# Moving the second gate product, the output product and the turn of the next input in an attention stage

## What is computed

```python
H, DK, DV, M = (16, 64, 128, 64)
x = layernorm(x)
q, k, v, g = x @ Wq, x @ Wk, x @ Wv, x @ Wg
s = clip(x @ Ws, -32, 32)
z = cumlogsumexp(s, axis=time);  p = exp(s - z)
# slots' keys: hk_t = hk_(t-1) * exp(z_(t-1) - z_t) + k_t p_t ;  ok_t = q_t . hk_t
pv = softmax(ok)
# slots' values: hv_t = hv_(t-1) * exp(z_(t-1) - z_t) + p_t v_t ;  o_t = pv_t . hv_t
o = o * rsqrt(mean(o * o) + EPS) * g_norm_weight * (g * sigmoid(g))
x_out = x_in + o @ Wo
```

## Time and profile before

| what | value |
|---|---|
| runs | 2952.86, 2950.38, 2964.53 us; median 2952.86 |
| the profiled execution's own time | 2954.36 us |
| its span, first to last instruction | 2952.5 us |
| mean granted TensorE clock over the span | 0.926 |
| TensorE matmuls busy | 2514.7 us, 85% |
| VectorE busy | 1756.5 us, 59% |
| GpSimd busy | 1258.2 us, 43% |
| ScalarE busy | 890.2 us, 30% |

### The profile page before, as it was taken

How to read it: one execution, slowest core, us unless ns; L and a number is a source line. 1 busy time by engine, 2 the same in 40 slices (tenths; PEclk the granted TensorE clock), 3 DMA queues, 4 the chain that set the end, 5 groups by cost and what they waited for, 6 DMA issues and landing times. The chain is left out here.

```text
span 2952.5 us, 46247 instructions
## 1 busy us (share of the span) xinstructions
PE 2514.7 (85%) x17244; PEld 2143.4 (73%) x17244; DVE 1756.5 (59%) x3538; ACT 890.2 (30%) x1886; POOL 1258.2 (43%) x1257
## 2 busy tenths in 40 slices
PE   6466499999999999999999999854654899796998
PEld 5444378888888888888888888754443678675777
DVE  5333267778787777777777777643222444464543
ACT  6222133333333333333333333253221222232322
POOL 2277634554444555555444455412883211242000
PEclk9588799999999999999999999855997899897999
DMA  6699600000000000000000000035995111111110
GB/s 219 172 255 236 132 11 19 5 15 19 19 9 15 15 19 19 5 16 19 19 8 15 16 19 12 3 124 144 217 217 110 61 58 35 43 57 44 36 35 30
DMA packets 210065, 186.21 MB, mean 63 GB/s; under 512 B 29280, under 2 KB 202304, under 8 KB 209344
## 3 DMA queue, kind: packets, MB, share of 16 engines
q1 hardware_dynamic: 180624, 133.83, 15.2%
q0 software_dynamic: 24576, 37.77, 6.9%
q10 hardware_dynamic: 4656, 11.80, 1.3%
HBM read 126.26 MB, written 61.52 MB: 64 GB/s over the span
## 5 line engine op out<-in xcount | busy, mean ns | idle before, releaser
L895 POOL TENSOR_TENSOR a_orstd<-a_ms,minus_half 128x8 f32<-128x8 f32 x64 | 106.3, 1661 | 637.4 <-DVE a_ms L1055 637.4
L1028 DVE TENSOR_TENSOR a_at<-a_psB,causal 128x384 f32<-128x384 f32 x512 | 260.6, 551 | 100.2 <-PE a_psB L1200 100.2
L875 POOL TENSOR_SCALAR a_pick<-a_index,lut_row 128x258 f32<-128x258 int32 x240 | 279.5, 1165 | 24.4
L1048 DVE RECIPROCAL a_rz<-a_rz 128x256 f32<-128x256 f32 x128 | 221.6, 1733 | 0.0
L616 PE MATMUL e_psX<-ident,e_xg 128*128 128x128 f32 x256 | 62.9, 333 | 177.5 <-DMA e_xg<-rows,slot_tok 177.4
L709 DVE TENSOR_TENSOR e_hT<-e_psH,e_sil 128x128 f32<-128x128 f32 x128 | 37.3, 292 | 272.6 <-ACT e_sil L677 272.5
L1578 DVE TENSOR_TENSOR f_hs<-f_psU,f_sil 128x512 f32<-128x512 f32 x96 | 66.2, 690 | 219.8 <-PE f_psU L1403 219.8
L616 PEld LDWEIGHTS e_psX<-ident,e_xg 128*128 128x128 f32 x256 | 32.1, 160 | 225.7 <-DMA e_xg<-rows,slot_tok 221.3
L878 POOL TENSOR_TENSOR a_found<-a_found,a_pick 128x258 f32<-128x258 f32 x240 | 177.6, 740 | 20.0
L1261 PE MATMUL a_psD<-a_v,a_at 128*128 128x128 f32 x1536 | 182.0, 275 | 0.0
L1261 PEld LDWEIGHTS a_psD<-a_v,a_at 128*128 128x128 f32 x1536 | 176.9, 192 | 0.1
(11 more groups left out here) (257 smaller groups left out, 7750.2 us busy)
## 6 DMA issues: line engine op xcount, KB each, us to landing
e_wg<-in_L_ffn_w_gate SPq DMA_DIRECT2D x128, 128.0 KB, 3.4
e_wu<-in_L_ffn_w_up SPq DMA_DIRECT2D x128, 128.0 KB, 3.7
e_wd<-in_L_ffn_w_down SPq DMA_DIRECT2D x128, 128.0 KB, 4.3
rows<-r_row SPq DMA_DIRECT2D x32, 320.0 KB, 3.1
stream_b<-r_zeros SPq DMA_DIRECT2D x11, 384.0 KB, 6.7
stream_c<-rows SPq DMA_DIRECT2D x33, 128.0 KB, 3.2
r_xt<-in_L_attn_hidden_states SPq DMA_DIRECT2D x16, 256.0 KB, 3.9
stream_a<-r_xt SPq DMA_DIRECT2D x16, 256.0 KB, 4.5
```

The lines of the kernel that those rows point to most:

```text
L875: nc.gpsimd.tensor_scalar(pick[:, :, :], index[:, :, :], float(c), w["lut"][:, c:c + 1], ALU.is_equal, ALU.mult).then_inc(picked, 1)
L895: nc.gpsimd.tensor_tensor(out=flat(orstd[:, :, :]), in0=ms[:, :], in1=cst["minus_half"][:, 0:TT * HQ], op=ALU.pow).then_inc(orstd_ok, 1)
L1028: nc.vector.tensor_tensor(out=at[:, h, :], in0=psB[h % 2][:, 0:3 * P], in1=cst["causal"][:, :, :].rearrange("p a i -> p (a i)"), op=ALU.mu ...
L1048: nc.vector.reciprocal(rz[:, a, :], rz[:, a, :]).then_inc(rz_ok, 1)
```

## The change

On TensorE, the turn of the next input goes from behind the first causal scores to between the first gate product and the second slot scores. The second gate product goes to behind the second slot scores, before the value sum. The output product goes from there to between the two pairs of causal scores, writes psC[0] in place of a bank of psA, and waits for the low part of lnT, since the turn also writes psC[0]. The slots' read waits for the adding of the output two rounds back. The gate's wait for that adding and the output's wait for the key go.

On VectorE, the moments of the next input are taken in the round of quarter 1 in place of 2, and the normalising in that of quarter 2 goes from behind the second reciprocal to where the moments stood. The subtraction for the low part goes from between the two gates to between the two reciprocals, and the adding of the output goes from there to behind the second gate.

On ScalarE, the copy of the high part goes from between the two gate tanhs to before the squares. On GpSimd, the 1/sqrt for the input goes from behind the look-ups of quarter 2 to directly behind the sum of the input in quarter 1, ahead of that round's look-ups.

```diff
--- before.py
+++ after.py
@@ -886,9 +886,8 @@
                     more = b + 1 < B
                     if q == 1 and more:
                         add_stream(b + 1)
+                        rstd_of_stream(b + 1)
                     look_up(b, range(4 * q, 4 * q + 4))
-                    if q == 2 and more:
-                        rstd_of_stream(b + 1)
                     if q == 0:
                         accumulator(b)
                     pool.wait_ge(ms_ok, n + 1)
@@ -968,6 +967,8 @@
                     if ahead:
                         key(n + 1)
                         turned_exps(n + 1)
+                        if (n + 1) % QPB == QPB - 1 and n + 2 < N:
+                            high_of_stream((n + 1) // QPB + 1)
                     for t in range(TT):
                         if t == 0:
                             act.wait_ge(ov_ps, n + 1)
@@ -976,8 +977,6 @@
                         nc.scalar.activation(sq[:, t * HQ * DV:(t + 1) * HQ * DV], psD[:, t, :], ACT.Square).then_inc(sq_ok, 1)
                     if ahead:
                         gate_tanh(n + 1, 0)
-                        if (n + 1) % QPB == QPB - 1 and n + 2 < N:
-                            high_of_stream((n + 1) // QPB + 1)
                         gate_tanh(n + 1, 1)
                 high_of_output(N - 1)
 
@@ -1009,13 +1008,13 @@
                                                 in1=oT[:, 0, 2 * a:2 * a + 2, :].rearrange("p a t -> p (a t)"),
                                                 op=ALU.subtract).then_inc(otl_ok, 1)
 
-                def add_output(n, bank):
+                def add_output(n):
 
                     dve.wait_ge(out_ps, n + 1)
                     dve.wait_ge(xacc_ok, n // QPB + 1)
                     if n > 0:
                         dve.wait_ge(acc_ok, n)
-                    nc.vector.tensor_tensor(out=xacc[:, :, :].rearrange("p t d -> p (t d)"), in0=psA[bank],
+                    nc.vector.tensor_tensor(out=xacc[:, :, :].rearrange("p t d -> p (t d)"), in0=psC[0],
                                             in1=xacc[:, :, :].rearrange("p t d -> p (t d)"), op=ALU.add).then_inc(acc_ok, 1)
 
                 def clip(m):
@@ -1086,6 +1085,8 @@
                     nc.vector.scalar_tensor_tensor(out=es[:, :], in0=sm[:, :], scalar=4.0 * EPS, in1=sm[:, :],
                                                    op0=ALU.mult, op1=ALU.mult).then_inc(es_ok, 1)
                     if q == 2 and b + 1 < B:
+                        normalise_stream(b + 1)
+                    if q == 1 and b + 1 < B:
                         moments_of_stream(b + 1)
                     dve.wait_ge(ezt_ps, n + 1)
                     nc.vector.tensor_tensor(out=flat(pzT[:, :, :]), in0=psC[0], in1=flat(rz[:, :, :]), op=ALU.mult).then_inc(pzt_ok, 1)
@@ -1099,12 +1100,9 @@
                     if ahead:
                         running_sum(n + 1, 1)
                         invert(n + 1, 0)
-                    if n > 0:
-                        add_output(n - 1, (n + 1) % 2)
-                    if ahead:
+                        if (n + 1) % QPB == QPB - 1 and n + 2 < N:
+                            low_of_stream((n + 1) // QPB + 1)
                         invert(n + 1, 1)
-                    if q == 2 and b + 1 < B:
-                        normalise_stream(b + 1)
                     dve.wait_ge(ov_ps, n + 1)
                     dve.wait_ge(tg_ok, TT * n + TT)
                     gated_output(n, 1)
@@ -1113,13 +1111,14 @@
                     if ahead:
                         masked(n + 1, (0, 1), at_ps, at_ok)
                         gate(n + 1, 0)
-                        if (n + 1) % QPB == QPB - 1 and n + 2 < N:
-                            low_of_stream((n + 1) // QPB + 1)
                         gate(n + 1, 1)
+                    if n > 0:
+                        add_output(n - 1)
+                    if ahead:
                         masked(n + 1, (2, 3), at_ps, at_ok)
                     squares(n)
                 low_of_output(N - 1)
-                add_output(N - 1, (N + 1) % 2)
+                add_output(N - 1)
 
             @block.tensor
             def _(pe):
@@ -1182,8 +1181,6 @@
                         pe.wait_ge(q_ok, m + 1)
                     else:
                         pe.wait_ge(k_ok, m + 1)
-                        if m > 1:
-                            pe.wait_ge(acc_ok, m - 1)
                     project("g", psA[(1 - m % 2) if t == 0 else m % 2], m, t, HQ * DV, g_ps)
 
                 def turn_exps(m):
@@ -1223,8 +1220,8 @@
 
                 def slots_read(n):
 
-                    if n > 0:
-                        pe.wait_ge(pzt_ok, n)
+                    if n > 1:
+                        pe.wait_ge(acc_ok, n - 1)
                     for a in range(NH):
                         pe.wait_ge(at_ok, HQ * n + 2 * a + 2)
                         for i, (t, j) in enumerate(((0, 0), (1, 0), (1, 1))):
@@ -1271,12 +1268,12 @@
                                                          o2[:, t, h * DV:(h + 1) * DV], ident)
                         mm.then_inc(ot_ps, 1)
 
-                def output(n, bank):
+                def output(n):
 
                     pe.wait_ge(otl_ok, NH * n + NH)
                     for t in range(TT):
                         for h in range(HQ):
-                            mm = split_matmul(nc, psA[bank][:, t * D:(t + 1) * D], [oT[:, part, h, t * P:(t + 1) * P] for part in range(2)],
+                            mm = split_matmul(nc, psC[0][:, t * D:(t + 1) * D], [oT[:, part, h, t * P:(t + 1) * P] for part in range(2)],
                                               [w["o"][part][:, n % QPB * HQ + h, :] for part in range(2)], h == 0, h == HQ - 1)
                     mm.then_inc(out_ps, 1)
 
@@ -1312,23 +1309,22 @@
                     scores_b(n, (0, 1))
                     if ahead:
                         gate(n + 1, 0)
-                    scores_b(n, (2, 3))
-                    if n > 0:
-                        if ahead:
-                            pe.wait_ge(k_ok, n + 2)
-                        else:
-                            pe.wait_ge(tg_ok, TT * n + TT)
-                        output(n - 1, (n + 1) % 2)
-                    over_j(n)
-                    if ahead:
-                        scores_a(n + 1, (0, 1))
                         if (n + 1) % QPB == QPB - 1 and n + 2 < N:
                             turn_stream((n + 1) // QPB + 1)
+                    scores_b(n, (2, 3))
+                    if ahead:
                         gate(n + 1, 1)
+                    over_j(n)
+                    if ahead:
+                        scores_a(n + 1, (0, 1))
+                    if n > 0:
+                        pe.wait_ge(lnTl_ok, min((n + 1) // QPB + (2 if (n + 1) % QPB == QPB - 1 else 1), B))
+                        output(n - 1)
+                    if ahead:
                         scores_a(n + 1, (2, 3))
                 turn_output(N - 1)
                 pe.wait_ge(acc_ok, N - 1)
-                output(N - 1, (N + 1) % 2)
+                output(N - 1)
         clear_semaphores(nc, mem)
 
 
```

More of the change, by code:

```diff
@@ L1314, in _ @@
                         gate(n + 1, 0)
+                        if (n + 1) % QPB == QPB - 1 and n + 2 < N:
+                            turn_stream((n + 1) // QPB + 1)
                     scores_b(n, (2, 3))
-                    if n > 0:
-                        if ahead:
-                            pe.wait_ge(k_ok, n + 2)
-                        else:
-                            pe.wait_ge(tg_ok, TT * n + TT)
-                        output(n - 1, (n + 1) % 2)
+                    if ahead:
+                        gate(n + 1, 1)
                     over_j(n)
@@ L1324, in _ @@
                         scores_a(n + 1, (0, 1))
-                        if (n + 1) % QPB == QPB - 1 and n + 2 < N:
-                            turn_stream((n + 1) // QPB + 1)
-                        gate(n + 1, 1)
+                    if n > 0:
+                        pe.wait_ge(lnTl_ok, min((n + 1) // QPB + (2 if (n + 1) % QPB == QPB - 1 else 1), B))
+                        output(n - 1)
+                    if ahead:
                         scores_a(n + 1, (2, 3))
```

## The result

| | before | after |
|---|---|---|
| median | 2956.86 us (17 runs) | 2945.55 us (17 runs) |
| ratio after/before | | 0.9958, 95% interval 0.9947 to 0.997 |
| span of the profiled execution | 2952.5 us | 2943.7 us |
| mean granted TensorE clock over the span | 0.926 | 0.938 |

The changed kernel is 0.42% faster: 12.4 us by the ratio (8.9 to 15.7 by its interval), 11.3 us by the medians, against 9.6 forecast. It is a real gain, but of the size that was called "within 0.5%". One of the 17 runs before took 3710.75 us, for a reason that nothing here shows; without it the median before is 2956.3.

What follows compares the result with a forecast made beforehand. TensorE's stream was taken to bound the attention stage. 15 x (0.69 - 0.05) = 9.6 us off the profiled 2954.4 gives 2944.8; the runs' median lies 1.5 lower, so 2943.3 us, range 2937 to 2956.

Steps and rivals of the forecast that it cites:

- (1): TensorE block seams after swapping second gate and output products: 0.45 us before and after, nothing; bounds 5.7 us either way.
- (2): lnT conversion chain, 1.82 us, gets 7.45 us of cover, so the 0.69 us wait goes; output product has 1.2 spare.
- (3): Turn of the next input between gate and scores: 0.44 us in place of 0.39, losing 0.05 in each of 15 rounds.
- (4): psC[0] as output bank: slots' read now waits for the output's adding, with 1.4 us spare; nothing.
- (5): Value sum starts 1.4 us sooner, 0.4 us behind the end of VectorE's masks; nothing.
- (6): Second causal scores wait for VectorE's masks of the first pair: 0.9 us spare in plain rounds, 0.4 with a turn.
- (7): VectorE's moments a round earlier, normalising in their place: at most 0.72 us in place of 0.94, 0.9 us spare.
- (8): GpSimd's chain at sample's end: store and xacc copy about 5 us later, fitting with 0.1 us, loads 0.5 spare; nothing.
- Blocked normalising: Rival: VectorE's normalising waits for GpSimd look-ups, 15 us back, 2958; chance 0.17 together with another wait eating the gain.
- Seams: Rival: TensorE block seams at one bound, 5.7 us cheaper 2937.6 or dearer 2949.0; chance 0.10, half on the fast side.
- VectorE the bound: Rival: masks for second causal scores over 0.9 us late; at 1.3 late 25 us less 9.6, 2968; chance 0.06.
- Another wait of the same size: Rival: a wait in GpSimd's sample-end chain or the lnT chain meets the gain, 2953; chance 0.17 with blocked normalising.

Runs made afterwards that it cites:

- experiment 6: Changed kernel with two more 128x512 reductions on VectorE ahead of the gated outputs in every round: 2967.31 us, ratio 1.0033.
- experiment 4: Changed kernel with statistics and 1/sqrt back in the round of quarter 2 and the normalising behind pzT: 2945.28 us, ratio 0.996.
- experiment 8: The changed kernel once more, unedited, on another chip than the run with the new order only in turn rounds: 2945.22 us, ratio 0.9963.
- experiment 7: Changed kernel, but in the last round VectorE takes the sum of squares before adding the previous round's output: 2944.24 us, ratio 0.9954.
- experiment 1: Changed kernel with the new order only in the 15 rounds with a turn, old order and psA bank in the others: 2948.23 us, ratio 0.9962.
- experiment 2: Changed kernel with the old order on TensorE, VectorE and ScalarE, keeping psC[0], early moments and early 1/sqrt: 2957.09 us, ratio 1.0.
- experiment 5: Changed kernel with GpSimd's copy into xacc moved behind the head scaling, about 4 us later: 2993.07 us, ratio 1.0122.
- experiment 3: Changed kernel with GpSimd holding its look-ups of quarter 2 until both normalisings are done: 2937.78 us in a single execution.

## Why the prediction was right, point by point

**The mechanism.** The wait for lnT's low part was the only thing in the loop that TensorE's stream could lose, and it went: 16 waits against one at the start. In the changed kernel the copy and the subtraction run while the value sum streams (ScalarE's timeline, then VectorE's):

```profile
1019.25 0.59 ACT L905 ACTIVATE a_lnT<-a_psC 128x512 fp32r<-128x512 f32 x1
```

```profile
1020.28 0.63 DVE L1001 TENSOR_TENSOR a_lnT<-a_psC,a_lnT 128x512 fp32r<-128x512 f32 x1
...
1023.62 1.01 DVE L1027 TENSOR_TENSOR a_at<-a_psB,causal 128x384 f32<-128x384 f32 x2
1024.55 1.28 DVE L1033 SCALAR_TENSOR_TENSOR a_tg<-a_tg,a_psA 128x512 f32<-128x512 f32 x2
1025.74 0.68 DVE L1017 TENSOR_TENSOR a_xacc<-a_psC,a_xacc 128x512 f32<-128x512 f32 x1
```

**(1) Seams** (from the last start of a block to the first of the next). Gate to value sum 1018.51 - 1018.28 = 0.23, output to scores 1025.15 - 1024.94 = 0.21, predicted 0.24 and 0.21. Plain rounds still came out 0.04 shorter: the output product's 24 matmuls with the seam behind them take 1025.15 - 1022.14 = 3.01, where (1) implied 2.96 + 0.09. That is 1.8 us in all, inside the bounds of 5.7.

**(2) The chain's cover.** The subtraction ends at 1020.91, the output product starts at 1022.14: 1.2 us spare, as worked out.

**(3) The turn.** Gate to turn to scores is 0.23 + 0.53 = 0.76 in place of one gate-to-scores seam of 0.33. The difference, 0.43, is the predicted 0.44, and it is what turn rounds take over plain ones (23.87 - 23.44).

**(4) and (5).** No slots' read waits for the adding, and one waits 0.3 for the masks, in the last round. The adding ends at 1026.42 for a slots' read at 1027.60, 1.2 us spare against 1.4. The value sum starts at 1018.51, 0.4 behind the end of the masks that it needs, as worked out:

```profile
1017.10 1.02 DVE L1027 TENSOR_TENSOR a_at<-a_psB,causal 128x384 f32<-128x384 f32 x2 [1.27 <-PE a_psB L1197]
```

**(6) Masks.** The first pair's end at 1024.63, for the second scores at 1025.15: 0.5 spare in a round with a turn against 0.4 predicted, and 1.1 against 0.9 in a plain one. Experiment 6 shows the smaller spare by its price.

**(7) Moments.** Their place costs nothing (experiment 4), as predicted. Nor does it gain. The two normalisings take 0.83 from start to start of the next instruction, where "at most 0.72" was counted, a bound made of the shortest and the typical of the earlier trace rows. The 0.9 us of spare hid the difference.

**(8) GpSimd's chain.** The copy starts 0.57 behind the slots' read and ends 0.1 ahead of the next GpSimd step, as forecast to 0.1 us. But "at nothing" missed its scatter. In two of the 15 rounds the chain was late; in one of them, the later by far, SP's queue, GpSimd, VectorE and TensorE read as follows:

```profile
1638.43 0.40 SPq L825 DMA_DIRECT2D x_att<-a_xacc  x1
```

```profile
1642.70 0.61 POOL L861 COPY a_xacc<-a_xab 128x512 f32<-128x512 f32 x1 [13.95 <-DMA x_att<-a_xacc]
...
1647.03 1.27 POOL L849 TENSOR_TENSOR a_xab<-a_xab 128x512 f32<-128x512 f32 x1
```

```profile
1648.34 0.75 DVE L988 BATCH_NORM_STATS2 a_bs<-a_xab 128x6 f32<-128x256 f32 x2 [1.19 <-POOL a_xab L849]
```

```profile
1650.00 0.71 PE L1196 MATMUL a_psB<-a_pzT,a_emT 64*128 64x256 f32 x4 [0.34 <-DVE a_pzT L1092]
```

The store took 4.2 us to land where the median is 2.2; the copy came 2 us late, the sum ended at 1648.30, and the scores waited 0.34. With the second late round that is about 0.6 of the 1.3 us above; the rest is mostly 0.07 us in ten of the rounds of quarter 0, which stands in no row of waits and stays open. In three other rounds the sum waited for the loads, 0.2 to 0.9 us, where about 0.5 was thought spare, and TensorE felt nothing. The late round is the one place in the loop where the change brought a new wait. In the second execution (experiment 8) there is none.

**The sum.** 9.6 us were forecast for the loop. 12.4 are there in the one execution and 10.0 in the other: 10.3 and 9.8 where 9.6 stood, 1.8 from plain rounds at "nothing" less 1.3 to 1.5, and in the first one 1.6 from the clock in the first two rounds. So the forecast of the loop was closer than the 12.4 makes it look. The rest of the measured gain lies in the last round, which the forecast took at nothing, and in the scatter, since the ratio's interval alone is 7 us wide: that the 11.3 us of the medians come near 9.6 is in part luck.

**The last round** was the worst-sized term: nothing, with 2 us either way, against 3.0 in this pair of executions. Before, the output product of the round stood ahead of the value sum, on the path and here at the lower granted level; TensorE's timeline of the kernel before, then of the changed one:

```profile
1896.89 0.58 PE L1401 MATMUL a_psA<-wo_high,a_oT 128*128 128x256 f32 x1
...
1901.97 1.28 PE L1261 MATMUL a_psD<-a_v,a_at 128*128 128x128 f32 x10
```

```profile
1887.38 3.77 PE L1258 MATMUL a_psD<-a_v,a_at 128*128 128x128 f32 x24
1890.91 0.37 PE L1397 MATMUL a_psC<-wo_high,a_oT 128*128 128x256 f32 x1
```

Before, 5.08 us lie between the output's start and the value sum's; the value sum is what everything after waits for. Now it goes first, and the output runs beside the gated outputs. The gain is less than 5.08 because VectorE's sum of squares then waited for the output's adding, which experiment 7 takes away. The estimate was made from 2.96, the product's length at full clock.

How much of the 3.0 is the order and how much the clock, the other executions show. The time is from the last slots' read to the start of the stage's last matmul, the clock the mean granted one from 9.6 to 33 us behind that slots' read:

| kernel | output in the last round | us | clock |
|---|---|---|---|
| before | ahead of the value sum | 35.6 | 0.65 |
| experiment 1 | ahead of the value sum | 33.8 | 0.65 |
| experiment 2 | ahead of the value sum | 32.5 | 0.79 |
| changed | behind it | 32.6 | 0.67 |
| experiment 8 | behind it | 33.0 | 0.66 |
| experiment 5 | behind it | 30.9 | 0.78 |
| experiments 3, 4, 6 | behind it | 30.4, 30.6, 30.3 | 0.85 |

In experiment 2 the output-to-value-sum distance is 2.93 in place of 5.08. At like clock the order is worth 0.8 to 3.0 us (1.6 at 0.78), which fits the 2 us of the estimate; the clock alone moves the round by as much.

**The rivals.** *Blocked normalising* did not come: the longest is 0.606, and nothing waits. The rule of the Trainium skill (SBUF — State Buffer, Who interferes with whom), that a tensor_scalar of VectorE in its two-port mode and a GpSimd instruction exclude each other for the whole instruction, would have delayed it here by 1.17 or 0.74 us. The traces show 0.08 at the median beside look-ups, and both normalisings of a round lie inside a single look-up (in the first round with a turn 445.28 to 446.18, inside a look-up of 1.22 us that started at 445.21). No row shows in which mode the instruction ran, so the traces decide against the delay here, not against the rule. Beside a GpSimd copy there is a delay, but the 0.97 of the prediction is too much: four instructions of that line at 2343.12 without a copy take 1.38, against the 2.09 of the earlier trace rows, so 0.71 was lost. *Seams* stayed within 0.04 of the value taken, on the cheap side. *VectorE the bound* needed it to come 0.9 us later than counted in plain rounds, and there it has 1.1 to spare; experiment 6 shows the place is real. *Another wait of the same size* did not come, but (8) is where it would have: experiment 5 prices the 4 us at 48 us, clock included.

## What to carry to other kernels

When one engine's stream is full, a wait in it is removed by putting other blocks of the same stream behind the producer, and what it brings can be read off as the wait less the change in seams. List the spare of every other chain that the move lengthens, and distrust one under half a microsecond that holds a transfer, since only its late side costs. Price a wait by more than its length: what runs behind it may run at a lower granted clock, as in experiment 5. Compare two traces only after reading the granted clock of both, stretch by stretch; the 1.6 us of the first two rounds looked like a gain. The rounds without steady state (first, last) follow their own path: read what each block there waits for, at the clock that is granted there.

## What the runs showed of the hardware

- The distance from a block's last matmul start to the next block's first depends on the pair: 0.12 from a 256-wide output product to the value sum, 0.21 to scores, 0.23 from a 512-wide gate to the value sum or the transposes, 0.33 from it to scores.
- The store of a sample (128x512) had landed after 2.2 us at the median of 15 and after 4.2 at the most, in a stage where the DMA engines were 5% busy on average. Before, the most was 2.5.
- VectorE's normalising takes 0.407 with GpSimd held and 0.49 at the median with its look-ups beside it, far from a full exclusion. An instruction of the same shape in a later stage took up to 1.118 beside a GpSimd copy and 0.41 at the median.
- In the last 26 us of the stage before (1893 to 1919 us), where TensorE waits for others again and again, the granted clock was 0.64, a mix of the levels of 1.2 and 2.4 GHz. 256-wide matmuls stood 0.21 us apart there instead of the 0.12 of the loop, so a block there can cost nearly twice what it does in the loop. Over ten executions the same part of the last round had a mean clock of 0.65 to 0.85.
- After a wait of 2.2 to 2.5 us in the loop the granted clock fell in eight of 14 rounds (0.83 or less over 10 us) and stayed at 1.00 in six, with the same instructions (experiment 5).
